# A vision-tower kernel with 15 routed experts: the second bias as rows of the sums, the second shared expert's down products behind the routed tiles, and a new order of GpSimd's multiplications

## The reference

```python
scores = softmax(xt @ gate_w.T)                       # 592 x 15
topk_w, topk_idx = top_k(scores, 3)                   # weights normalised
h = einsum('td,efd->etf', xt, fc1_w) + fc1_b          # 15 experts, 2 x 256 hidden
a = gelu(h[..., F:]) * h[..., :F] * geglu_mult
yexp = einsum('etf,edf->etd', a, fc2_w) + fc2_b       # the second bias, per expert
y = einsum('etd,te->td', yexp, comb)                  # comb: 3 weights per token
ys = (gelu(gs) * xs * s_geglu_mult) @ s_fc2_w.T + s_fc2_b   # shared, 512 hidden
out = layernorm(xt + y + ys)
```

## Time and profile before

| | |
|---|---|
| median of 3 runs | 211.78 us (211.69 to 212.29) |
| the profiled execution | 211.57 us, of which the span is 209.8 us |
| granted PE clock | 0.992 of full speed |
| busy: PE, DVE, ACT, POOL | 95%, 54%, 45%, 58% of the span |
| HBM | 29.27 MB read, 4.06 MB written |

### The profile page before, as it was taken

How to read it: one execution, slowest core, us unless ns; L and a number is a source line. 1 busy time by engine, 2 the same in 40 slices (tenths; PEclk the granted TensorE clock), 3 DMA queues, 4 the chain that set the end, 5 groups by cost and what they waited for, 6 DMA issues and landing times.

```text
span 209.8 us, 4431 instructions
## 1 busy us (share of the span) xinstructions
PE 199.2 (95%) x1559; PEld 124.7 (59%) x1559; DVE 113.2 (54%) x313; ACT 94.4 (45%) x219; POOL 121.5 (58%) x148
## 2 busy tenths in 40 slices
PE   7999998999998899999998999999999999999981
PEld 4776676678786675776775753355444555445630
DVE  6685697868863444264799953642344332231034
ACT  2004565477868373564557762333332433235024
POOL 0040079869989857929999877216665552347100
PEclk9999999999999999999999999999999999999996
DMA  6999999960000399922220034228985321112483
GB/s 199 391 416 314 402 415 417 425 270 0 6 3 3 97 379 376 417 83 64 78 71 22 0 100 108 78 92 304 366 326 164 92 75 53 50 50 91 145 248 116
DMA packets 13822, 38.32 MB, mean 183 GB/s; under 512 B 2697, under 2 KB 4618, under 8 KB 13802
## 3 DMA queue, kind: packets, MB, share of 16 engines
q1 hardware_dynamic: 11786, 32.54, 42.4%
q0 software_dynamic: 2016, 5.51, 8.4%
HBM read 29.27 MB, written 4.06 MB: 159 GB/s over the span
## 4 chain that ended last, share of the span: by engine, by line
PE 77%; DVE 8%; DMA 6%; issue 2%; ACT 2%; POOL 2%; SPq 1%; POOLq 0%; DVEq 0%; ACTq 0%
PE ps L383 66%; PE ps L1874 3%; PE ps L1672 2%; DMA wres<-y_dram 2%; PE ps L1914 2%; PE ps L1687 2%; DMA embed_sb<-embed 1%; POOL y_dram L668 1%; DMA embed_sb<-x_dram,gather_i 1%; DMA y_dram<-ln_mem,dest_i 1%; PE ps L1603 1%; PE ps L1530 1%; DVE over L1270 1%; POOL embed_sb L659 1%; ACT ln_mem L905 1%
## 5 line engine op out<-in xcount | busy, mean ns | idle before, releaser
L383 PE MATMUL ps<-wres,cT 128*64 (+1 forms) x360 | 63.1, 469 | 0.0
L383 PEld LDWEIGHTS ps<-wres,cT 128*64 128x64 f32 (+1 forms) x360 | 25.4, 131 | 27.7 <-issue 20.5
L668 POOL DMA_INDIRECT y_dram<-ln_mem,dest_i x21 | 20.6, 982 | 26.8 <-ACT ln_mem L875 23.4
L426 POOL TENSOR_TENSOR wres<-wres,fac_mem 128x512 f32<-128x512 f32 x22 | 27.2, 1271 | 4.3 <-DVE ln_rs L1033 4.3
L659 POOL DMA_INDIRECT embed_sb<-x_dram,gather_i x21 | 20.3, 968 | 8.2 <-issue 5.2
L1406 DVE TENSOR_TENSOR fac_mem<-ps,h 128x256 f32<-128x256 f32 x21 | 8.9, 423 | 24.0 <-ACT h L869 24.0
L869 ACT ACTIVATE h<-ps 128x256 f32<-128x256 f32 x21 | 8.0, 383 | 28.5 <-PE ps L383 28.5
L383 PE MATMUL ps<-h,stage 128*128 128x296 f32 x64 | 18.2, 422 | 0.7 <-DVE xn L1384 0.6
L1413 DVE COPY cT<-ps 128x256 f32<-128x256 f32 x21 | 8.8, 424 | 15.6 <-PE ps L383 15.6
L875 ACT ACTIVATE ln_mem<-ps 128x256 f32<-128x256 f32 x21 | 8.0, 383 | 15.8 <-PE ps L383 15.8
L383 PEld LDWEIGHTS ps<-h,stage 128*128 128x128 f32 x64 | 11.6, 190 | 5.4 <-DVE xn L1384 1.0
(11 more groups left out here) (215 smaller groups left out, 379.9 us busy)
## 6 DMA issues: line engine op xcount, KB each, us to landing
wres<-experts SPq DMA_DIRECT2D x15, 768.0 KB, 13.5
fac_mem<-experts SPq DMA_DIRECT2D x11, 256.0 KB, 8.1
wres<-ut SPq DMA_DIRECT2D x3, 768.0 KB, 8.8
embed_sb<-embed SPq DMA_DIRECT2D x5, 416.0 KB, 5.6
stage<-shared SPq DMA_DIRECT2D x2, 771.0 KB, 16.4
stage<-wres SPq DMA_DIRECT2D x2, 512.0 KB
wres<-y_dram SPq DMA_DIRECT2D x2, 512.0 KB, 4.2
wres<-y_dram SPq DMA_DIRECT2D x2, 384.0 KB, 6.3
```

The lines of the kernel that those rows point to most:

```text
L383: return nc.tensor.matmul(o, w, x, start=start, stop=stop)
L426: nc.gpsimd.tensor_tensor(w1(e, c), w1(e, c), row, ALU.subtract).then_inc(less_done, 1)
L668: pool.indirect_dma_start(out=y_dram[:, :], out_offset=bass.IndirectOffsetOnAxis(ap=dest_i[:, column(i):column(i) + 1], axis=0), in_=ys[:, ...
```

## The change

1. **Bias.** The matrix `mix` and the rows read back get 17 more partitions (96 to 112): the weights of all experts per token from `comb_dram` (4 small DMAs on SP behind `comb17`'s), and the second biases, copied 16 times side by side by one DMA on SP that waits for the last `second`. `whole_sums` is 113 rows deep instead of 96, and the bias product stays for the last token tile alone.
2. **Rows of the last token tile.** They are read by one DMA of ACT's queue (32 partitions x 9 KB) instead of by SP.
3. **Shared expert.** `down` is made for e = 0 alone, so one less in each half; both units of e = 1 are kept in `a_late`, and their down products are made token by token at the end.
4. **The last routed tile.** Behind second(15): second(16), second(17), gated_transposed(18), (19), first(20), second(18), gated_transposed(20), second(19), second(20); ACT's and DVE's order follows.
5. **POOL.** The multiplications of experts 0 and 1 are moved behind group 2 and ahead of the wait for `ln2.rs`, those of experts 2 and 3 behind group 3 and ahead of the wait for `ln3.rs`. The subtraction of expert 14 waits for the end of `slots` (`rt` at 11), and expert 4's multiplication follows it.

```diff
+KB = KS + NE
-LESS_TO = (3, 6, 9, E)
+LESS_TO = (3, 6, 9, E - 1)
+SLOTS_END = 11
...
-        comb17 = sb("comb17", [NE, T])
+        comb17 = sb("comb17", [NE, LAST])
...
-        a_late = h1_mem[:, 2 * F:2 * F + T]
+        a_late = (pair_mem[:, 2 * TOPK * TT * E:2 * TOPK * TT * E + T], h1_mem[:, 2 * F:2 * F + T])
...
         def read_rows(eng, t):
             cols = slice(PC * t, PC * (t + 1))
-            rows = P if cols.stop <= HELD else KS
-            eng.dma_start(yr[0:rows, cols], y_sums[0:rows, cols]).then_inc(ld_y[t], 16)
-            if cols.stop < HELD < cols.stop + PC:
-                rest = slice(cols.stop, HELD)
-                eng.dma_start(yr[KS:P, rest], y_sums[KS:P, rest]).then_inc(ld_y[t], 16)
+            eng.dma_start(yr[0:KS, cols], y_sums[0:KS, cols]).then_inc(ld_y[t], 16)
...
-            sp.dma_start(comb17[:, :], comb_dram[:, 0:T]).then_inc(ld_c17, 16)
+            sp.dma_start(comb17[:, :], comb_dram[:, (TT - 1) * P:T]).then_inc(ld_c17, 16)
+            for j in range(PC):
+                sp.dma_start(mix_rows[KS:KB, j], comb_dram[:, 0:(TT - 1) * P].rearrange("e (t j s) -> e t j s", t=TT - 1, j=PC)[:, :, j]) \
+                    .then_inc(ld_c17, 16)
...
-            sp.wait_ge(st_zero, 16)
+            sp.wait_ge(y2_mm, NT)
+            sp.dma_start(yr[KS:KB, 0:YC], b2_sb[:, :].unsqueeze(1).to_broadcast([NE, YC, D])).then_inc(ld_y[0], 16)
             rows_written(sp)
...
             for e in range(LESS_TO[0], LESS_TO[1]):
                 less_first(pool, e)
+            for e in range(2):
+                expert_mult(e)
             pool.wait_ge(ln2.rs, 2)
             sums(1)
             for e in range(LESS_TO[1], LESS_TO[2]):
                 less_first(pool, e)
+            for e in range(2, 4):
+                expert_mult(e)
             pool.wait_ge(ln3.rs, 1)
             for e in range(LESS_TO[2], LESS_TO[3]):
                 less_first(pool, e)
-            for e in range(MULT_POOL):
+            pool.wait_ge(rt, SLOTS_END)
+            for e in range(LESS_TO[3], E):
+                less_first(pool, e)
+            for e in range(4, MULT_POOL):
                 expert_mult(e)
...
             warm(ACT.Sqrt)
+            act.wait_ge(st_zero, 16)
+            rows_written(act)
+            act.dma_start(yr[KS:P, YC:YC + HELD], y_sums[KS:P, 0:HELD]).then_inc(ld_y[1], 16)
...
-                if 2 <= k < 5:
+                if 2 <= k < 4:
                     down(0, k - 2)
                 if k == 7:
...
                     down(1, 0)
-                    down(1, 1)
...
-            down(1, 2)
-            for j in range(0, NT, 2):
+            down(1, 1)
+            for j in range(0, NT - 1, 2):
...
+            second(NT - 5)
+            second(NT - 4)
+            gated_transposed(NT - 3)
+            gated_transposed(NT - 2)
+            first(NT - 1)
+            second(NT - 3)
             gated_transposed(NT - 1)
-            second(NT - 3)
             second(NT - 2)
             second(NT - 1)

-            pe.wait_ge(ld_c17, 16)
             for t in range(TT):
                 rows = P if t < TT - 1 else LAST
                 o = ps[0:rows, SUM_BANK[t], 0:D]
-                mm(o, comb17[:, t * P:t * P + rows], b2_sb[:, :], True, False)
+                for j in range(FC):
+                    mm(o, a_late[j][:, t * P:t * P + rows], stage[:, 1, W1C + j * D:W1C + (j + 1) * D], j == 0, False)
+                if t == TT - 1:
+                    pe.wait_ge(ld_c17, 16 * (PC + 1))
+                    mm(o, comb17[:, :], b2_sb[:, :], False, False)
                 for c in range(DC):
                     mm(o[:, c * P:(c + 1) * P], hs[:, c, t * P:t * P + rows], ident, False, False)
-                mm(o, a_late[:, t * P:t * P + rows], stage[:, 1, W1C + D:WC], False, False)
             def whole_sums(t):
-                pe.wait_ge(ld_y[t], 32 if t == 1 else 16)
+                pe.wait_ge(ld_y[t], 32 if t < 2 else 16)
                 for j in range(PC):
-                    last = mm(ps[SUMS * j:SUMS * (j + 1), SUM_BANK[t], 0:D], mix[:, j, t], yr[0:KS, PC * t + j],
+                    last = mm(ps[SUMS * j:SUMS * (j + 1), SUM_BANK[t], 0:D], mix_rows[:, j, t], yr[0:KB, PC * t + j],
                               False, True)
```

More of the change, by code:

```diff
@@ L279, in vit_tower_kernel @@
         mix_end = mix_at + PC * (TT - 1) * SUMS
-        mix = emb_mem[0:KS, mix_at:mix_end].rearrange("p (j t s) -> p j t s", j=PC, t=TT - 1)
+        mix_rows = emb_mem[0:KB, mix_at:mix_end].rearrange("p (j t s) -> p j t s", j=PC, t=TT - 1)
+        mix = mix_rows[0:KS]
         mix_last = emb_mem[KS:P, mix_end:mix_end + PC * TOPK * SUMS].rearrange("p (j k s) -> p j k s", j=PC, k=TOPK)
@@ L879, in _ @@
             warm(ACT.Gelu)
-            for j in range(0, NT, 2):
-                for i in range(j, min(j + 2, NT)):
+            for j in range(0, NT - 1, 2):
+                for i in range(j, j + 2):
                     gate(i)
@@ L889, in _ @@
                     tile_out(i)
+            tile_out(NT - 5)
+            tile_out(NT - 4)
+            gate(NT - 1)
             for i in range(NT - 3, NT):
@@ L1289, in choose @@
             def choose():
-                dve.wait_ge(rt, 11)
+                dve.wait_ge(rt, SLOTS_END)
                 pick_of(0, jump[:, :].rearrange("p (t e) -> p t e", t=TT))
@@ L1451, in _ @@
                         mixing_last(k)
+            gated_in(NT - 3)
+            gated_in(NT - 2)
+            gated(NT - 1)
             gated_in(NT - 1)
@@ L1811, in slot_table, with down @@
                 last.then_inc(tab_mm, 1)
-            def down(n, u):
-                e, j = u // FC, u % FC
-                pe.wait_ge(t1_done, 4 * n + u + 1)
-                if u == 0:
+            def down(n, j):
+                pe.wait_ge(t1_done, 4 * n + j + 1)
+                if j == 0:
                     pe.wait_ge(scaled, FC * NS)
                 for c in range(DC):
-                    last = mm(ps[:, 2 * n + c, 0:HT], stage[:, e, W1C + j * D + c * P:W1C + j * D + (c + 1) * P],
-                              a_sh[:, u], u == 0, u == 2)
+                    last = mm(ps[:, 2 * n + c, 0:HT], stage[:, 0, W1C + j * D + c * P:W1C + j * D + (c + 1) * P],
+                              a_sh[:, j], j == 0, j == FC - 1)
                 last.then_inc(y_mm, 1)
```

14 lines of the change are left out of this document (7 added, 7 removed).

## The result

The changed kernel takes **225.44 us** (median of 4 runs, 225.29 to 225.65), the kernel before 212.03 beside it (4 runs, 211.69 to 212.75): ratio 1.064, 95% interval 1.061 to 1.067, so 13.4 us slower. The forecast was 211.4 us, with a range of 209.9 to 213.1: the result lies far outside. The profiled executions show the same: 225.58 us (span 223.6) against 211.57 (span 209.8).

A forecast was written before the change was run, and what follows sets the result against it. It took PE to bound the kernel nearly everywhere, with DVE's routing and two roots as other stretches. Terms 0.6 + 0.2 - 0.65 + 0 - 0.55 = -0.4 us took the median of 211.78 to 211.4 us, range 209.9 to 213.1.

The forecast's parts named there:

- The last tiles: End of the kernel: last scatters 0.65 us earlier, worth -0.55 us (-0.6 to 0); copied bias 0, at most +0.6.
- Rival (d): At the end, copied bias or ACT's DMA delays rows or last scatters by 0.6 us: 212.0 us, no change; chance 0.10.
- Rows and bias: Small DMAs on SP, rows' depth and bias products at the end: 113 rows cost PE nothing, 2.76 off, 2.65 on; 0.
- First root: Four multiplications behind group 2, three beside DVE's 13 root steps, delay the root PE waits for: +0.6 us (0 to 1.1).
- Second root: Four multiplications behind group 3 delay DVE's root by about 0.5 us; PE takes it 0.3 later: +0.2 (0 to 0.8).
- rival (b): Multiplications beside the roots' 13 steps cost 0.38 us each, roots +1.1 and +0.8: slower by 1.2, 213.0 us; chance 0.20.
- The routing: DVE's routing: 1.65 us from two freed steps, 0.9 from multiplications gone, 1.9 lost to expert 14's subtractions: -0.65 (-2.6 to +0.5).
- The down products: One less in each half, 1.16 us, ahead of PE's waits for DVE and gather; PE only waits longer: 0.
- rival (c): Beside the roots, each POOL multiplication holds DVE for its whole length, over 0.6 us each: 214.2 us; chance 0.03.

The follow-up runs named there:

- copy as 16 and 1: The changed kernel with its copy of the biases cut into two DMAs, of 16 partitions and 1 partition; 219.43 us against 214.11 for the kernel before, ratio 1.026.

## Why the prediction was wrong

**The step that failed** is the end of "The last tiles", where the copied bias is costed: its price "no row shows", then 272 KB are set against the 4.75 us of the DMA that ended the read-back "behind 1 MB", and "I take 0, at most +0.6". It sized the copy by its bytes. The row that it took is that of a small DMA of 32 KB which landed behind two reads of 128 partitions, and these use all engines (a share of 1.00 in that kernel from 198 to 199 us). The runs show about 25 GB/s for the 17 partitions, 11 us more than without the copy (13.4 less 2.1), and 3.2 us even on all engines. The bound of 0.6 had no row behind it. An upper bound from the profile was to be had: 272 KB at a sixteenth of the 413 GB/s that the weights' loads reach are 10.8 us. Rival (d) named the right place, the copy or ACT's DMA delaying rows and last scatters, and gave it the same 0.6.

**A second step failed too**, in "Rows and bias": the rows' reads over 96 partitions were not costed at all, and the clock was not thought of. The reads cost 1.2 us of transfer, and the clock that PE has behind its waits up to 2.0 to 2.5 us more: it was halved for all of the last 42 products behind a wait of 1.39 us, and for a part of them already behind two of 0.55 and 0.52. The products ahead of the sums, "0 taken", became 0.9 us shorter (192.75 to 200.31 against 191.74 to 200.16 before). It is worth nothing where the rows end last; there it only makes PE idle longer.

How the loss divides, then, as far as single profiles allow (13.8 us, by their spans). The stretches are those ahead of the last scatter's issue, from there to the first sum, and from there to the end of the span:

| kernel | last scatter's issue | to the first sum | to the end |
|---|---|---|---|
| changed | 193.94 | 18.16 | 11.5 |
| copy as 16 and 1 | 196.25 | 9.74 | 11.5 |
| no copy | 196.08 | 7.91 | 10.3 |
| no copy, rows read as before | 196.09 | 6.72 | 10.4 |
| before | 193.60 | 6.56 | 9.6 |

The first column can be compared only between the first row and the last, 0.3 us, and among the other three. One engine instead of 16 costs 8.4 us, all of it waiting, since the clock is low at the end with both. The copy on 16 engines costs 3.0, of which 1.2 lie in the last stretch and are the clock's. The new reads cost 1.2 and nothing there. Of the last 1.3 us, 0.3 lie ahead of the last scatter, 0.2 before the first sum and 0.8 in the last stretch, where the 42 products take 4.67 instead of 3.31 us at a partly low clock.

**The other steps held in the main**, and they were small:
- *First root*, forecast +0.6: PE waits 1.02 instead of 0.19 us, +0.83. Four of the 13 steps are held, and take 0.38 to 0.53 instead of 0.20 to 0.24. *Second root*, +0.2: PE reaches it 1.21 us later than the earlier trace rows, so +0.4. With both, +1.2 instead of +0.8, on the way to rival (b), but short of it. Alone on the kernel before, the multiplications cost 0.4 (medians) to 0.9 (ratio) net.
- *The routing*, forecast -0.65: the first gather comes at 120.00, 0.86 later than before, of which 1.21 are the roots: -0.35. The two freed steps gave 1.71 (forecast 1.65), the three L1262 lost 1.87 (2.86 against 0.98 by their own times, forecast 1.9); what was too high was the 0.9 for multiplications gone, of which 0.5 came: the scan L1222 and the mask ahead of it, free before, each took 0.27 us longer beside subtractions.
- *The down products*, 0: their time turned into waits of PE, 1.21 us for `h` at 113.97, and 0.70 and 0.79 for two gathers. Right, and with its cover gone as was said.
- *The last tiles*, the scatters 0.65 earlier: the last is 0.34 later, though PE's products end 1.0 later, 0.67 gained. Right, also alone on the kernel before (-0.45 to -0.6). What it is worth in the changed kernel, where the copy decides when the first sum starts, no run shows.
- *The hold*, rival (c), a whole multiplication: it did not come. Eight multiplications beside two chains of 13 steps cost 1.2 us together, 0.15 each, where that rival had 0.65. Against the rule of the Trainium skill that was quoted with it, the trace disagrees for multiplications (0.53 us at most for a step of 0.24, beside multiplications of 0.92) and agrees for subtractions (1.31 for a step of 0.23, beside one of 1.27).

What stays open: why the copy from ACT's queue is slower still, and why a copy on 16 engines keeps them busy until 200 us at 94 to 190 GB/s and so makes the last scatter 2 us late.

## What to carry over

Before a DMA is called small, look at the outermost dimension on both sides, not at its bytes: here 17 partitions ran on one engine, and scatters and reads of other queues, which need that engine too, landed late with it. Price such a DMA from a row of the same shape or by bytes over a sixteenth of the full rate, and split it into a part of 16 partitions and a rest. Where the end of a kernel waits for a transfer, PE's idle time can be paid twice, the second time through the clock of what follows (here 1.39 us of it, and 2.0 more).

## What was not expected of the hardware

- **A wait that the traces of the first comparison don't have.** In both of these PE runs through from 127 to 134 us. On the four chips of the experiments ACT, DVE and POOL start nothing for 1.2 to 2.7 us from about 130 us on, and PE stops too and loses 1.2 to 2.0 us: in 14 of 15 profiles (in the other, in which POOL is late with the gathers, the three engines pause but PE doesn't stop). It would be most of the 2 us by which the kernel before is slower there; that kernel itself was not profiled there, so this is an inference, and so is it that the chip decides. Its cause the profile doesn't show, and it was not tried.
- **The clock within the routed tiles.** In the three profiles in which PE's wait is 1.96 to 2.03 us the granted clock falls, and the eight products behind it take 2.43 to 3.11 us instead of 1.94; behind waits of up to 1.87 us they took 1.94. PE's timeline and a stretch of the new reads with added products:

```profile
133.26 3.11 PE L383 MATMUL ps<-wres,cT 128*64 x8 [1.96 <-DVE fac_mem L1405]
```

```profile
134.00:135.00 1.00, 1.00 (x4) 0.25 (x2) 0.86 (x5) 0.00 (x0) 0.00 (x0) 0.50 0.45 131
```

  In the run with expert 14's subtraction behind `slots` the same happens from 126 to 129 us, behind waits of 1.86 and 0.91 us for gathers. A clock that falls in some executions and not in others would make two groups of runs from one kernel, as seen there. The mean granted clock of each run fits: 0.992 in the three runs of 214.1 to 214.3 us, 0.977 to 0.989 in the six slower ones. Only one of these was profiled, so where it fell in the others is not shown.
